# Three float32r matmuls of upper and lower parts for the first feed-forward layer

## The reference, cut to what matters

```python
# attention 1 (x is the block's state after a layer norm, 256 features; w1 is 1024 x 256)
ff = jnp.tanh(x @ w1.T + b1) @ w2.T + b2
# attention 3 (fc1_w is 256 x 256)
z = jnp.maximum(x2 @ fc1_w.T + fc1_b, 0.0) * mask0
z = (z @ fc2_w.T + fc2_b) * mask0
# attention 5 (ffn_w1 is 1024 x 256)
h = _ln(q, g_out, b_out)
h = jax.nn.relu(h @ ffn_w1.T + ffn_b1) @ ffn_w2.T + ffn_b2
```

## Time and profile before

| | |
|---|---|
| median of three runs | 3154.09 us (3152.81 to 3174.43) |
| the profiled execution's own time | 3151.89 us |
| its span, first to last instruction | 3150.1 us |
| mean granted TensorE clock | 0.975 |
| busy share: TensorE, VectorE, ScalarE, GpSimd | 94%, 53%, 41%, 18% |
| stages on the span | attention 1 about 600 to 1060 us; attention 3 about 1600 to 2095; attention 5 about 2510 to 3150 |
| products of the first feed-forward layer (L690) | 1152 records, busy 285.8 us |

### The profile page before, as it was taken

The page is one execution under the profiler, slowest core; times in us unless marked ns, Lnnn a source line. Parts: engine busy times, 40 slices in busy tenths (PEclk is TensorE's granted clock), DMA queues, the critical chain, the costliest instruction groups (busy, mean ns, idle before and its releaser), DMA issues.

```text
span 3150.1 us, 66716 instructions
## 1 busy us (share of the span) xinstructions
PE 2947.0 (94%) x27925; PEld 2060.9 (65%) x27968; DVE 1683.8 (53%) x3261; ACT 1289.8 (41%) x1809; POOL 562.8 (18%) x519
## 2 busy tenths in 40 slices
PE   8999999999999999899888988889999999999998
PEld 5666766677777777666655655566566666666666
DVE  5656565544444445555567777665555544443431
ACT  1333333444444433443444444444444544444443
POOL 0111111212222222211113333331111110000000
PEclk9999999999999999999998999899989999999999
DMA  2200000010000000100101101001000010000000
GB/s 90 86 28 28 27 23 16 29 32 23 24 22 22 25 15 23 36 24 26 33 30 39 32 23 32 16 22 62 22 22 28 24 33 28 26 25 21 28 22 14
DMA packets 78073, 92.76 MB, mean 29 GB/s; under 512 B 14378, under 2 KB 59578, under 8 KB 77779
## 3 DMA queue, kind: packets, MB, share of 16 engines
q1 hardware_dynamic: 77778, 88.49, 8.9%
HBM read 39.93 MB, written 4.19 MB: 14 GB/s over the span
## 4 chain that ended last, share of the span: by engine, by line
PE 85%; DVE 8%; ACT 3%; issue 3%; DMA 1%; SPq 1%; DVEq 0%; ACTq 0%
PE ps_nat L465 24%; PE ps_misc L555 9%; PE ps_pv L625 9%; PE ps_misc L690 9%; PE ps_misc L712 7%; PE ps_misc L580 5%; PE ps_misc L662 4%; DVE mx L918 4%; PE ps_misc L636 2%; PE ps_nat L469 2%; ACT pt L769 2%; PE ps_misc L550 2%; PE ps_st L486 2%; PE ps_misc L680 2%; PE ps_st L482 2%
## 5 line engine op out<-in xcount | busy, mean ns | idle before, releaser
L769 ACT ACTIVATE pt<-ps_st 128x1024 f32<-128x1024 f32 (+1 forms) x768 | 759.5, 989 | 1112.4 <-PE ps_st L482 599.1
L918 DVE TENSOR_REDUCE mx<-ps_nat 128x4 f32<-128x1024 f32 x640 | 782.0, 1222 | 782.0 <-PE ps_nat L465 670.0
L465 PE MATMUL ps_nat<-k,q 17*128 17x256 f32 (+1 forms) x6144 | 867.4, 400 | 117.5 <-DVE mx L918 80.9
L482 PE MATMUL ps_st<-q,k 18*128 18x256 f32 (+1 forms) x6144 | 866.7, 400 | 0.1
L465 PEld LDWEIGHTS ps_nat<-k,q 17*128 17x128 f32 x6144 | 522.1, 188 | 362.4 <-issue 176.0
L482 PEld LDWEIGHTS ps_st<-q,k 18*128 18x128 f32 x6144 | 516.0, 188 | 2.8 <-issue 1.7
L625 PE MATMUL ps_pv<-pt,vaug 128*32 128x256 f32 (+1 forms) x6144 | 415.6, 390 | 0.0
L1046 POOL TENSOR_TENSOR rstd<-var,half_pow 128x2 f32<-128x2 f32 x144 | 101.9, 708 | 1402.4 <-DVE var L820 1402.0
L690 PE MATMUL ps_misc<-xF,weights 128*128 128x256 f32 x1152 | 285.8, 392 | 17.8 <-ACT xF L783 17.8
L1054 POOL TENSOR_TENSOR xn<-xn,tiles 128x512 f32<-128x512 f32 x128 | 164.1, 1282 | 663.2 <-DVE xn L824 663.2
L625 PEld LDWEIGHTS ps_pv<-pt,vaug 128*32 128x32 f32 x6144 | 163.7, 111 | 180.4 <-issue 110.7
(11 more groups left out here) (105 smaller groups left out, 3191.4 us busy)
## 6 DMA issues: line engine op xcount, KB each, us to landing
q<-plain SPq DMA_DIRECT2D x320, 64.0 KB, 2.6
k<-plain SPq DMA_DIRECT2D x320, 64.0 KB, 2.5
weights<-in_weights SPq DMA_DIRECT2D x19, 512.0 KB, 4.0
cT<-in_ctx_t SPq DMA_DIRECT2D x32, 256.0 KB, 2.8
cn<-in_ctx SPq DMA_DIRECT2D x32, 256.0 KB, 2.9
xT<-in_x_t SPq DMA_DIRECT2D x16, 256.0 KB, 3.8
xn<-in_x SPq DMA_DIRECT2D x16, 256.0 KB, 2.9
out<-xn SPq DMA_DIRECT2D x16, 256.0 KB, 2.0
```

What stands on the lines that cost most here:

```text
L465: return nc.tensor.matmul(ps_nat[:, j, hf, 0:keys], lhs, rhs, start=hf == 0, stop=last)
L482: return nc.tensor.matmul(ps_st[:, j, kh, 0:S - q0], lhs, rhs, start=kh == first, stop=last)
L769: nc.scalar.activation(pt[:, g % PT_SLOTS, :, 0:used], ps_st[:].rearrange("p j a b -> p j (a b)")[:, :, 0:used], ACT.Exp, scale=SCALE).the ...
L918: last = nc.vector.reduce_max(out, ps_nat[:], AX)
```

## The change

The weights of the first layer and its input are split on VectorE into an upper part in the format float32r and a lower part, the difference, also in float32r. TensorE then computes upper x upper, upper x lower (of the input) and lower (of the weights) x upper in place of the one fp32 product, into the same bank. New events `wsp` split the weights once in each of attentions 1, 3 and 5 (four pieces of 512 columns, in attention 3 one piece of two times 256). VectorE now serves `xff` too: it waits until ScalarE has written `xF`, casts it to `xF_hi` (L989 of the new kernel) and subtracts to `xF_lo` (L990), and the first `ff1` of a unit waits for that (`xF_split`). For room in memory, `vflip` becomes a view of `vT` and `bias_f` one of `plain`.

```diff
+        if a in (1, 3, 5) and n % B == 0:
+            for k in range(1 if a == 3 else 4):
+                add(8 * n + 2 + 2 * k, "wsp", n, k)
...
-        bias_f = sb("bias_f", [1, 1024])
...
+        xF_hi = sb("xF_hi", [P, 2, S], F32R)
+        xF_lo = sb("xF_lo", [P, 2, S], F32R)
+        up_hi = sb("up_hi", [P, 2, DF], F32R)
+        up_lo = sb("up_lo", [P, 2, DF], F32R)
...
+        bias_f = plain[0:1].rearrange("p a s -> p (a s)")
         vaug = sb("vaug", [P, 2, 2, H, 32])
-        vflip = sb("vflip", [P, 2, 512])
+        vflip = vT[:].rearrange("p r a s -> p r (a s)")
...
                     elif kind == "ff1":
                         if i == 0:
-                            wait_out(pe, ("xff", n, 0))
+                            pe.wait_ge(xF_split, nth(("xff", n, 0)))
+                            if u == 0:
+                                pe.wait_ge(up_split, nth(("wsp", n, 0 if a == 3 else 3)))
                         bank = open_bank(e)
-                        wu = w("u" + str(a), D if a == 3 else DF)
                         for c in range(2):
                             ch = 2 * i + c
                             for dk in range(2):
-                                last = nc.tensor.matmul(bank[:, c * S:(c + 1) * S], wu[:, dk, ch * P:(ch + 1) * P],
-                                                        xF[:, dk, :], start=dk == 0, stop=dk == 1)
+                                hi, lo = up_hi[:, dk, ch * P:(ch + 1) * P], up_lo[:, dk, ch * P:(ch + 1) * P]
+                                out = bank[:, c * S:(c + 1) * S]
+                                nc.tensor.matmul(out, hi, xF_hi[:, dk, :], start=dk == 0, stop=False)
+                                nc.tensor.matmul(out, hi, xF_lo[:, dk, :], start=False, stop=False)
+                                last = nc.tensor.matmul(out, lo, xF_hi[:, dk, :], start=False, stop=dk == 1)
                         filled(e, last)
...
                         dst = xT[:, rot] if kind == "xtr" else xF[:]
+                        if kind == "xff" and nth(e) > 1:
+                            act.wait_ge(xF_split, nth(e) - 1)
...
+                    elif kind == "wsp":
+                        dve.wait_ge(w_loaded[a], 16 * len(w_pieces(a)))
+                        wu = w("u" + str(a), D if a == 3 else DF)
+                        for dk, lo in (((0, 0), (1, 0)) if a == 3 else ((i // 2, 512 * (i % 2)),)):
+                            part = slice(lo, lo + (D if a == 3 else 512))
+                            link(nc.vector.tensor_copy(up_hi[:, dk, part], wu[:, dk, part]))
+                            last = nc.vector.tensor_tensor(up_lo[:, dk, part], wu[:, dk, part], up_hi[:, dk, part].bitcast(F32),
+                                                           ALU.subtract)
+                        last.then_inc(up_split, 1)
+                    elif kind == "xff":
+                        wait_out(dve, e)
+                        link(nc.vector.tensor_copy(xF_hi[:], xF[:]))
+                        nc.vector.tensor_tensor(xF_lo[:], xF[:], xF_hi[:].bitcast(F32), ALU.subtract).then_inc(xF_split, 1)
```

More of the change, by code:

```diff
@@ L28 @@
 F32 = mybir.dt.float32
+F32R = mybir.dt.float32r
 BF16 = mybir.dt.bfloat16
@@ L280, in block_kernel @@
         ff3_done, msk_done = sem("ff3_done"), sem("msk_done")
+        up_split, xF_split = sem("up_split"), sem("xF_split")
         stored = sem("stored")
@@ L336, in _ @@
             def _(sp):
-                sp.dma_start(bias_f[:], t["qk_row"]).then_inc(bias_in, 16)
+                sp.dma_start(bias_f, t["qk_row"]).then_inc(bias_in, 16)
                 for e in win.order:
@@ L832, in _ @@
                 for part in range(3):
-                    nc.vector.tensor_copy(bias_b[32 * part:32 * part + 1, :], bias_f[:]).then_inc(bias_made, 1)
+                    nc.vector.tensor_copy(bias_b[32 * part:32 * part + 1, :], bias_f).then_inc(bias_made, 1)
                     if part < 2:
                         dve.wait_ge(bias_made, 3 + 2 * part)
-                        nc.vector.tensor_tensor(bias_f[:], bias_f[:], bias_b[32 * part:32 * part + 1, :],
+                        nc.vector.tensor_tensor(bias_f, bias_f, bias_b[32 * part:32 * part + 1, :],
                                                 ALU.subtract).then_inc(bias_made, 1)
```

## The result

| | before | after |
|---|---|---|
| median of four runs each | 3153.45 us (3148.14 to 3174.43) | 3208.44 us (3205.86 to 3223.86) |
| the profiled execution's own time, and its span | 3151.89, 3150.1 us | 3207.12, 3205.3 us |
| mean granted TensorE clock | 0.975 | 0.956 |

The ratio is 1.0171, with a 95% interval of [1.0139, 1.0202]: the change makes the kernel 1.7% slower. The forecast was 3192 us, within 3138 to 3232.

The account below looks back on a forecast made before the run. TensorE, busy for 94% of the span, was taken to bound the kernel. From 3151.9 us, steps 1 to 3 gave -4.5 and the clock +44: 3191.4, say 3192 us, range 3138 to 3232.

Parts of the forecast that it names:

- 2 attention 1: Attention 1: the input's split delays VectorE's next work, L997, for which TensorE waits, by 0.1 us x 16: +1.6 us.
- 2 attention 3, 12 units: Attention 3: the context's mask stands behind the split, so mask and TensorE's transposes start 2.29 us late, 12 times: +27.5 us.
- 2 attention 5: Attention 5, before the first ff1: all of the input's split is on the path, 1.22 us x 16: +19.5 us.
- 4 clock, attention 3: Attention 3: TensorE's clock falls in 11 places at 2.6 us, 29 us, less about 10 us that falls already cost.
- 4 clock, attention 5: Attention 5: TensorE's clock falls at the longer idle time before ff1, 14 places at 1.8 us: 25 us.
- Step 1, the products: ff1 in attentions 1, 3, 5: three float32r parts at 0.109 us replace 0.432 us, for 576 products: -60.5 us.
- Step 2, the split of the input: VectorE, 48 times at xff: cast 0.43 us, subtraction 0.69, in all 1.22 from xF's end to ff1; cost differs by attention.
- Step 3, the split of the weights: VectorE, nine pieces of 1.18 us, each between two maxima: half of the 10.6 us bound, +5 us.
- Step 4, the clock: Attentions 3 and 5: longer idle times at xff bring TensorE to half clock in nine in ten of 28 places: +44 us.
- Stalls without falls: Rival, attentions 3 and 5: the stalls come but the clock does not fall; 3147 us, no change; chance 0.26.
- Stalls given back: Rival, rest of a unit in attentions 3 and 5: half the idle time is given back, no new fall; 3105 us; chance 0.08.
- A float32r part that isn't one quick read: Rival, ff1 products: a part takes 0.19 us (load not hidden) or 0.216; 3331 or 3377 us; chance 0.08.

Follow-up runs that it names:

- The kernel with the products alone: Against the changed kernel: input not split, ScalarE writes the upper part, which also replaces the lower in the second product; weights still split; 3114.45 us, ratio 0.9852.
- the first experiment: Against the changed kernel: attention 3's split of the input put behind VectorE's masking of the context, all else the same; 3149.51 us, ratio 0.996.

## Why the prediction was right or wrong

The mechanism was right, down to the place of each wait. Three sizes were wrong: the products, and the clock in attentions 3 and 5. The last two, +17 and -19 us off, cancel, and that was luck.

| step | forecast | measured | from |
|---|---|---|---|
| 1 products | -60.5 | -41 | 0.360 us a product, not 0.327: 0.072 x 576 |
| 2 attention 1 | +1.6 | about 0 | units 1.2 us shorter, 16 products save 1.15 |
| 2 attention 3, 12 units | +27.5 | +26 | wait 0.25 to 2.40 |
| 2 attention 5 | +19.5 | +19 | wait 1.11 to 2.30 |
| 4 clock, attention 3 | +19 | +36 | eleven units, net of what fell before |
| 4 clock, attention 5 | +25 | +6 | 6.9 less the 0.6 of steps 1 and 2, one execution |

The measured terms sum to +46; of the 9 us that are left, most lie in the last four units of attention 3 and in attention 4 (+3.8), where I had 2.4 and nothing. No run places them further.

- **Step 1, the products, is the step that failed**, by 19 us. I took bf16's pace, 0.109 us for 256 columns, for float32r's; it is 0.120. Three times in each of 576 products that is 19 us. That this is about what lies between 3192 and 3208 is in part chance: the step for the weights (+5) left no trace, and 9 us are unplaced. The upper bound (0.216) was far off, and so were the 0.19 for a load that isn't hidden: loads of 190 ns run beside matmuls that start every 0.12.
- **Step 2, the split of the input**, held. The cast takes 438 ns, forecast 430, the subtraction 692. The Trainium skill's rule on double rate (VectorE: DVE Perf Modes, "The perf-mode tier table") thus holds for a float32r output too, by this trace's 438 ns. Moving the split behind the mask took the wait away (35.0 to 7.7 us); with the wait and its falls went 50 us.
- **Step 3, the split of the weights**, +5 us, wasn't measured by itself. The kernel with the products alone keeps it and shows no sign of a cost, within an interval wider than the term. The stretch up to the first `xF`, which became 4.3 us shorter, says nothing of it: it ended anywhere between 618.6 and 629.1 us in the traces of the float32r kernels, which differ little there.
- **Step 4, the clock**, came to 42 us in place of 44, but not in the places that I gave. In attention 3 every unit of the twelve has half clock behind the wait, mostly for 6.8 us, and 3.6 us a unit were lost, the upper end of the earlier trace rows and not 2.6; filling the idle time brought them back. In attention 5 I took nine in ten to fall; 6 of 16 did, and the two among the first eleven units cost 1.4 us each (42.1 us beside 40.7). The +6 is that one execution's: the two others with the same attention 5 took 6 and 9 us more over the eleven units. Its clock of 0.99 came near to the 1.00 that I had named as a sign of being wrong. The rest of a unit in attention 3 has several more idle times; that they prolong a fall is my reading and wasn't tried.
- **The rule of the Trainium skill** (TensorE: Matmul & The Clock Gate, "A second HAM failure mode: psum-queue depth-cycling") agrees with attention 3, where all twelve places fall, and not with attention 5, where ten of 16 idle times of 2.3 us are followed by a clock of 1.00.
- **Rivals.** Stalls without falls: not in attention 3; nearly what happened in attention 5. Stalls given back: no, the wait before the scores is 81.0 us, 80.9 before. A float32r part that isn't one quick read: no; 10% slower, not 74%.

What stays open: why the clock falls at only some of attention 5's equal idle times (with waits of 1.2 us, seven units of eleven in one kernel and two in another), while the same kernel's executions lie up to 1% apart (3129.93 us at a mean clock of 0.976 to 3161.24 us at 0.963 for the first experiment); and whether it is the columns or the loads that make float32r a tenth slower than bf16.

## What to carry to other kernels

Where a step is added on an engine with time to spare, look up what stands behind it in that engine's order, and whether the bound engine waits for that next: here the same 1.2 us of work was free in attention 1 and cost a unit 5 us in attention 3. Price an idle time of TensorE by the clock too: in attention 3 it took more (3.6 us a unit) than the wait had grown (2.15). And read the gain of a cheaper matmul from distances of starts of that very format, or keep a tenth of doubt on it.

## What the hardware showed that I had not expected

- Matmuls of 256 columns behind one another start every 0.109 us in bf16 and every 0.120 in float32r; 512 float32r columns take 0.24. The Trainium skill has one pace for a number of columns (TensorE: Matmul & The Clock Gate, "Back-to-back issue gap"): by its formula, which it gives for an isolated matmul, 0.109 and 0.216 us. The bf16 rows agree, though they stand in a stream; the float32r rows are a tenth above, and the measurement decides.
- A load of 128 columns of weights lasts 190 ns in four-byte formats and 98 in bf16, at full clock. The Trainium skill says two things of it (TensorE: Matmul & The Clock Gate, "Weight-path perf modes — Fast Weight Load (FWL) and DoubleRow"): in its text on fp8, that a load goes by columns and not by bytes; in its table, that a fast load reads 32 bits at a time, two bf16 numbers, with no gain for fp32. The two groups here differ, as the table has it.
- 18 matmuls without a use, in an idle time that stays, made the kernel faster: ratio 1.0049 in place of 1.0171.
